# A graph attention phase with one masked leaky score array, a mask made on ScalarE, and a new order on all engines

## The reference, cut to what matters

```python
h = relu(layernorm(x)); h = h + emb_table[node_type]
for t in range(3):
    xw = h @ W[t]; a_s = xw @ att_src[t]; a_d = xw @ att_dst[t]
    e = leaky_relu(a_s[src] + a_d[dst], 0.2)            # edges of type t only
    m = max(segment_max(e, dst), leaky_relu(a_s + a_d))
    w = exp(e - m[dst]); w_self = exp(leaky_relu(a_s + a_d) - m)
    out += (segment_sum(w * xw[src]) + w_self * xw) / (segment_sum(w) + w_self) + bias[t]
x = x + out
x = x + update(segment_sum((relu(layernorm(x))[src] @ dW + db) * filters(edge_attr)))
```

## Time and profile before

| what | value |
|---|---|
| median of 3 runs | 4670.54 us (4664.35 to 4681.23) |
| profiled execution: its time, its span | 4672.4 us, 4670.4 us |
| mean granted TensorE clock | 0.633 |
| busy: PE, PEld, DVE, ACT, POOL | 89%, 69%, 56%, 27%, 69% |
| attention phase, first to last look at a unit's maximum | 131.2 us to 2429.3 us |

### The profile page before, as it was taken

The page is one execution under the profiler, slowest core; times in us unless marked ns, Lnnn a source line. Parts: engine busy times, 40 slices in busy tenths (PEclk is TensorE's granted clock), DMA queues, the critical chain, the costliest instruction groups (busy, mean ns, idle before and its releaser), DMA issues. The chain is left out here.

```text
span 4670.4 us, 64104 instructions
## 1 busy us (share of the span) xinstructions
PE 4157.6 (89%) x18574; PEld 3219.4 (69%) x18575; DVE 2604.0 (56%) x6278; ACT 1242.0 (27%) x3966; POOL 3241.2 (69%) x3261
## 2 busy tenths in 40 slices
PE   7899999999999999999987689888888899888998
PEld 5676767767777777777766567776676677767776
DVE  6777777777777777777774333333333333333333
ACT  4433333333333333333331111111111111111111
POOL 3777777777777777777740577777777777777774
PEclk9656565566665556655666666666666666666667
DMA  2222222222222222222224222222222222222223
GB/s 80 50 50 48 48 48 48 48 48 48 48 48 48 48 47 48 48 48 48 48 29 130 66 73 74 73 73 74 73 74 72 74 74 73 74 73 74 73 74 75
DMA packets 215747, 288.25 MB, mean 62 GB/s; under 512 B 136194, under 2 KB 143930, under 8 KB 215723
## 3 DMA queue, kind: packets, MB, share of 16 engines
q0 software_dynamic: 105472, 222.39, 21.0%
q1 hardware_dynamic: 110250, 65.57, 5.1%
HBM read 277.81 MB, written 9.81 MB: 62 GB/s over the span
## 5 line engine op out<-in xcount | busy, mean ns | idle before, releaser
L54 POOL DMA_INDIRECT ae_xg<-table,ae_idx x1620 | 1677.2, 1035 | 640.9 <-issue 456.2
L54 POOL DMA_INDIRECT ce_xg<-table,ce_idx x1620 | 1534.1, 947 | 499.8 <-issue 493.4
L1042 DVE TENSOR_TENSOR ce_ps_f<-ce_ps_f,ce_fb 128x768 f32<-128x768 f32 x270 | 260.9, 966 | 1288.9 <-PE ce_ps_f L995 1288.9
L1014 PE MATMUL ce_ps_h<-ce_ea,ce_fw 50*128 50x384 f32 x1080 | 638.1, 731 | 247.1 <-DMA ce_ea<-in_edge_attr 246.6
L551 PE MATMUL ae_ps_a<-ae_e,ae_xg 128*128 128x96 f32 x3240 | 772.0, 402 | 63.5 <-DVE ae_e L662 63.5
L995 PEld LDWEIGHTS ce_ps_f<-ce_fw,ce_hid 128*128 128x128 f32 x3240 | 642.9, 301 | 239.5 <-issue 239.0
L551 PEld LDWEIGHTS ae_ps_a<-ae_e,ae_xg 128*128 128x128 f32 x3240 | 651.0, 293 | 164.0 <-DVE ae_e L662 88.1
L975 ACT ACTIVATE ce_hid<-ce_ps_h,ce_fb 128x768 f32<-128x768 f32 x270 | 243.1, 900 | 1782.8 <-PE ce_ps_h L1014 1782.8
L995 PE MATMUL ce_ps_f<-ce_fw,ce_hid 128*128 128x128 f32 x3240 | 715.9, 403 | 0.0
L512 ACT ACTIVATE ae_e<-ae_e,ae_sc 128x96 f32<-128x96 f32 x1620 | 459.7, 362 | 957.2 <-DVE ae_e L654 957.2
L555 PE MATMUL ae_ps_d<-ae_e,cst 128*1 128x96 f32 x3240 | 551.4, 356 | 0.0
(11 more groups left out here) (141 smaller groups left out, 3654.8 us busy)
## 6 DMA issues: line engine op xcount, KB each, us to landing
ce_ea<-in_edge_attr SPq DMA_DIRECT2D x270, 150.0 KB
ae_xg<-table,ae_idx POOLq DMA_INDIRECT x1620, 2.6
ce_xg<-table,ce_idx POOLq DMA_INDIRECT x1620, 2.6
fa_inv_den<-rden SPq DMA_DIRECT2D x7, 1344.0 KB, 7.6
ae_idx<-in_src SPq DMA_DIRECT2D x276, 3.0 KB, 1.6
ce_idx<-in_src SPq DMA_DIRECT2D x276, 3.0 KB, 1.6
table<-pr_rows POOLq DMA_DIRECT2D x7, 462.0 KB, 4.1
pr_x<-in_x SPq DMA_DIRECT2D x7, 448.0 KB, 3.3
```

The costliest lines, as they stand in the source:

```text
L54: eng.indirect_dma_start(out=out, out_offset=None, in_=table[:, :], in_offset=bass.IndirectOffsetOnAxis(ap=idx, axis=0)).then_inc(done, 16)
L1014: last = nc.tensor.matmul(ps_h[:, k * 512:k * 512 + H], fw1[:, :], ea[:, s % XS, k * H:(k + 1) * H], start=True, stop=True)
L1042: nc.vector.tensor_tensor(filt, filt, fb2[:, :].unsqueeze(1).to_broadcast([P, CH, D]), ALU.add).then_inc(s_bias, 1)
```

## The change

Three things change in the attention phase, and nothing in the other phases.

First, there is one score array. `e` = leaky(sc + dst - off) is made once per unit; the maximum is the maximum of this array, and the exponential is that of this array less the new maximum. ACT writes sc + dst into PSUM (`ps_y`, L538, six instructions, PSUM to PSUM), DVE subtracts `off` in place (L677), ACT makes 0.8 relu of it into `upper` (L529, one instruction over 576 numbers), DVE adds 0.2 of the array (L682), reduces it to `high` (L687), and later adds minus the maximum (L709); ACT takes one exponential over all 576 numbers (L519). Foreign keys stand at about -1e30 throughout, so nothing is masked after the exponential. PE spreads only the destination's score (L610) and one row with the new maximum and the rise side by side (L621, one matmul of 192 columns), and spreads the highest score without adding the destination's (L615).

Second, ACT makes `off`: the square of 2^50 (iota - key), six instructions per unit (L546), each with its bias column chosen by a register; `start_pass` writes the keys in that form (`less_key`, f32). The denominators' matmuls (L597) write into the bank of the sums.

Third, all four streams are ordered anew. On PE, a step holds the highest row, the maxima and the sums of unit n - 2, the denominators of n - 3 in two halves, the target row of n and the transpose of n - 1.

```diff
         @block.scalar
-                    for c in range(CH):
-                        nc.scalar.activation(by_chunk[b][:, c, :], by_chunk[b][:, c, :], ACT.Exp, bias=sc2[:, b, c:c + 1])
-                    act.wait_ge(s_fall, n)
-                    nc.scalar.activation(rescale[:, b, :], ps_d[b][:, KEYS:2 * KEYS], ACT.Exp).then_inc(s_e, 1)
+                    nc.scalar.activation(e[:, s % 3, :], e[:, s % 3, :], ACT.Exp).then_inc(s_e, 1)
+
+                def rescales(n):
+
+                    act.wait_ge(s_less, n)
+                    nc.scalar.activation(rescale, rescale, ACT.Exp).then_inc(s_rescale, 1)
+
+                def uppers(n):
+
+                    act.wait_ge(s_masked, n)
+                    nc.scalar.activation(upper[:, :].rearrange("p (h k) -> p h k", h=2), scores, ACT.Relu, scale=1.0 - SLOPE).then_inc(s_upper, 1)
...
+                    for c in range(CH):
+                        last = nc.scalar.activation(off[:, s % 2, c, :], h.iota, ACT.Square, bias=keys[:, c:c + 1], scale=STEP)
...
         @block.tensor
+                def maxima(n):
+
+                    pe.wait_ge(s_rise, n)
+                    nc.tensor.matmul(ps_m[:, 0:2 * KEYS], h.less_row32[0:64, :], rise[:, :, :].rearrange("p a k -> p (a k)"),
+                                     start=True, stop=True).then_inc(s_less, 1)
...
         @block.vector
+                def subtract(n, s):
+
+                    dve.wait_ge(s_rescale, n)
+                    nc.vector.tensor_tensor(by_chunk[s % 3], by_chunk[s % 3], less_max.unsqueeze(1).to_broadcast([P, CH, KEYS]),
+                                            ALU.add).then_inc(s_sub, 1)
```

More of the change, by code:

```diff
@@ L521, in turn @@
-                        if not (first and s < 2):
-                            act.wait_ge(s_sum, n - 2)
-                        act.wait_ge(s_dst, n)
-                        act.wait_ge(s_score, n)
-                        for c in range(CH):
-                            last = nc.scalar.activation(by_chunk[b][:, c, :], ps_c[b][:, 0:KEYS], ACT.Relu, bias=sc[:, b, c:c + 1])
-                        last.then_inc(s_pre, 1)
-                turns(act, turn)
-                exps((r + 1) * NU, SL - 1)
+                        n = (r * TURNS + i) * SL + s + 1
@@ L532, in _ @@
+                n = (r + 1) * NU
+                rescales(n - 1)
+                uppers(n)
+                exps(n - 1, SL - 2)
+                rescales(n)
+                exps(n, SL - 1)
         @block.tensor
@@ L560, in turn @@
                     for s in range(SL):
-                        n, b = (r * TURNS + i) * SL + s + 1, s % 2
-                        lag1 = not (first and s < 1)
-                        pe.wait_ge(s_high, n)
-                        nc.tensor.transpose(ps_t[0:KEYS, 0:P], high[:, :], h.ident).then_inc(s_turned, 1)
-                        nc.tensor.matmul(kv(ps_c[b][:, 0:KEYS]), h.ones[0:1, :], state[0:1, :, bass.ds(base[s], W)], start=True, stop=True)
-                        nc.tensor.matmul(kv(ps_c[b][:, KEYS:2 * KEYS]), h.slope[0:1, :], state[0:1, :, bass.ds(base[s], W)], start=True, stop=False).then_inc(s_dst, 1)
@@ new lines, in turn @@
+                        lag1, lag2, lag3 = (not (first and s < k) for k in (1, 2, 3))
+                        if lag2:
+                            highest_row(n - 2)
+                        if lag3:
+                            totals(n - 3, s - 3, range(0, CH // 2))
+                        if lag2:
+                            maxima(n - 2)
+                        if lag3:
+                            totals(n - 3, s - 3, range(CH // 2, CH))
+                        targets(n, base[s], first and s == 0)
@@ L583, in _ @@
+                        if lag2:
+                            sums(n - 2, s - 2, first and s < 4)
+                        if lag1:
+                            turned(n - 1)
                 pe.wait_ge(key_ready, r + 1)
@@ L665, in scale_sums @@
-                def scale_sums(n, s, base, fresh):
+                    new, fall = rise[32:33, 0, :], rise[32:33, 1, :]
+                    if not fresh:
+                        dve.wait_ge(s_max, n - 1)
+                    dve.wait_ge(s_z, n)
+                    nc.vector.tensor_tensor(kv(new), kv(ps_z[32:33, 0:KEYS]), m, ALU.max).then_inc(s_new, 1)
+                    dve.wait_ge(s_new, n)
+                    nc.vector.tensor_tensor(kv(fall), kv(new), m, ALU.subtract).then_inc(s_rise, 1)
```

244 lines of the change are left out of this document (117 added, 127 removed).

## The result

| | median us | lowest to highest | ratio to before (95%) |
|---|---|---|---|
| before, same chip | 4670.4 | 4664.35 to 4681.23 | |
| changed | 4537.5 | 4533.58 to 4541.97 | 0.971 (0.969 to 0.973) |

The change is 133 us faster, where 36 were forecast (4634), inside the range but 97 us off. The profiled execution took 4533.6 us with a span of 4531.9.

A forecast was written before the change was run, and what follows sets the result against it. The prediction took TensorE's stream at 1.2 GHz as the present bound (8.54 us a step) and a ring of waits as the new one: 8.27 + 0.09 + 0.03 = 8.39 us, giving 4634 us, range 4510 to 4712.

The forecast's parts named there:

- the ring: Attention-phase chain of waits from transpose through DVE, TensorE and ACT back to transpose, priced at 8.27 us at 1.2 GHz.
- sums twice 1.53 = 3.06: TensorE's sums matmuls ahead of the transpose, priced as two halves of 1.53 us each, 3.06 us.
- the reserve: Allowance of 0.03 us added to each attention step for errors in the six handovers between engines, giving 8.39 us.
- the head of a turn: DVE's register load at each turn's start, said to stick out about 0.55 us in six steps, 0.09 a step.
- the second rival: Slower: longer waits ahead of highest row and sums, clock low; 8.83 us a step, 4750 us, or 4710 at two thirds; chance 0.12.
- TensorE's own stream: TensorE's matmuls and transpose in one attention step, said to total 7.3 us at 1.2 GHz, against 8.6 before.
- The clock: TensorE was to stay at 1.2 GHz in nearly all of the attention phase, granted clock near 0.50.
- The first rival: TensorE's clock keeps rising as often as before (granted 0.60): step 8.0 us, 146 us less, 4528 us; chance 0.22.
- Its signs: Attention-phase profile readings expected if right: clock 0.50 to 0.52, TensorE's two waits, L687 starts 8.4 us apart, POOL waiting longer.
- POOL's floor: POOL's gathers with their issue take 7.81 us a unit, so no step averages less; 4480 us the least.
- What stays under cover: DVE's and ACT's other work in a step, 5.5 and about 5.0 us busy, said not to set the step.
- the convolution: The phase outside attention, priced at no change since none of its instructions moved.

The follow-up runs named there:

- e1: The changed kernel with TensorE's sums again in two halves of three matmuls, the target row between them: 4742.95 us, ratio 1.0145 to the kernel before.
- e14: The kernel before with both halves of its sums (L551) in one run behind the maxima L579 and L580: 5070.88 us, ratio 1.0856.
- e3: The changed kernel with TensorE's register load at a turn's head moved to just ahead of the first target row: 4519.2 us, ratio 0.9661.
- e4: The changed kernel with the exponential as six instructions of 96 numbers instead of one of 576: 4634.48 us, ratio 0.9908.
- e13: The changed kernel with the mask made on VectorE in two instructions of 288 numbers, not ACT's six L546: 4534.85 us, ratio 0.9701.
- e11: The changed kernel with TensorE's order as in e12, VectorE's order left as it was: 4634.49 us, ratio 0.9894.
- e12: The changed kernel, TensorE reordered with denominators in one run straight before sums, VectorE's leaky array and maximum ahead of merge and scale: 4388.55 us, ratio 0.9371.
- e10: The kernel of e12 with TensorE's register load moved to just ahead of a turn's first target row: 4386.22 us, ratio 0.9366.
- e5 to e8: Kernels of e13, e10, e12 with e13's mask, and e11, on a chip taking 5556 us for the kernel before: 5499.5, 5442.1, 5445.9, 5447.9 us.

## Why the prediction was wrong

**The step that failed** is the term of the ring "sums twice 1.53 = 3.06". They measure 2.67 us. The 1.53 was read from a half that stood between other matmuls, and doubling it charged the break between two halves that the new order does not have. e1 splits the difference: put back as halves, the sums take 2.90; one run saves 0.23 of it. The rest, 0.16, is the change to the next instruction: the last half takes 1.38 ahead of the transpose and 1.52 ahead of the target row, so the 1.53, read ahead of L555, was too dear there as well. In the kernel before the same step shows (e14): 2.81 us for one run ahead of L555. 0.39 us a step is 105 us, a little more than the miss: with 0.02 for the other terms and 0.03 for the reserve, less 0.08 for the head of a turn, the step came out 0.36 us shorter than forecast, and 0.36 x 270 = 97 us.

The other terms, with what they measured:

| term | priced | measured |
|---|---|---|
| transpose to L691, L691, handover | 0.48, 0.29, 0.06 | 0.46, 0.29, 0.05 |
| highest row, half of the denominators | 0.51, 1.00 | 0.51, 1.05 |
| maxima to their end, rescale | 1.02, 0.23 | 1.00, 0.23 |
| subtraction, exponential | 0.75, 0.65 | 0.76, 0.68 |
| three handovers, last handover | 0.12, 0.10 | 0.11, 0.05 |
| sums | 3.06 | 2.67 |
| ring | 8.27 | 7.86 |
| head of a turn, a step | 0.09 | 0.17 |
| reserve for handovers | 0.03 | 0 |
| step | 8.39 | 8.03 |

7.86 + 0.17 is 8.03, and so is (2296.0 - 135.6)/269. The steps with a turn's head take 8.85 us in the mean, 0.99 over the ring. **The head of a turn** was priced with VectorE's load alone, 0.55 us where 0.66 stuck out; TensorE's own load adds 0.47 us in half of the turns (the second rival's place, without its size), and e3 takes that back. The head was too cheap by 0.08 us a step, which hid part of the error in the sums.

**TensorE's own stream** was forecast at 7.3 us, and 7.86 less the two waits of 0.38 and 0.18 is 7.30. That agreement is luck: the denominators took 2.10 instead of 2.0, the maxima 0.94 to the next start instead of 0.81, the target row 0.67 instead of 0.5, and the sums 0.39 less than priced. The maxima's price per column was read from L1014, in another phase, and it was too low.

**The clock** was called rightly: 0.50 throughout. The first rival, a clock that keeps rising, gave 4528 us and came closest to the time, and it is wrong: the phase has not one stretch at 2.4 GHz. A time near a rival's is no evidence for it; the granted clock is. The prediction's reason for the low clock, that no dense stretch of sums and denominators is left, fits the other runs: with the denominators cut in two by the maxima (e1, e3, e4, e13) the granted clock of the attention phase is 0.50, and where denominators and sums stand back to back it is 0.62 (e11) and 0.67 (e12). No run changed that stretch and nothing else.

**Its signs.** TensorE waits 0.38 us ahead of L615 (0.5 said) and 0.18 ahead of L591 (0.4 to 0.5 said); L687's starts are 8.03 us apart (8.4 said); ACT is early at L524, 3.19 us. POOL's wait for L591 was to grow and fell, from 154.8 us to 61.2.

**The second rival** needed 0.90 for the exponential and 0.15 for the last handover; they are 0.68 and 0.05. **POOL's floor** of 7.81 us a unit was wrong as well, without effect at a step of 8.03: it took the gathers' 1026 ns as theirs, and 82 ns of it was VectorE's two-operand work. At 7.49 it became the bound as soon as the ring was shorter (e12). **What stays under cover** held: the mask costs nothing on either engine, neither as six short activations of ACT nor as VectorE's 0.92 us (e13). The maximum L687 had less room than said: it ended at 1412.98, 0.26 us ahead of the transpose, where the prediction left 0.8. And the convolution did not move (clock 0.6 to 0.7 after the phase, as before).

Where the 133 us came from, as far as shown: a ring of 7.86 us sets the step instead of TensorE's full stream of 8.6 us. Taking single parts out of the changed kernel costs 0.77 us a step for the unbroken sums outside the target row (e1, 206 us), 0.36 for the single exponential (e4), and nothing for the mask's move (e13). These prices hold inside the new order and do not add up to the gain over the old one, which no experiment took apart. What the second level of the clock was worth to the kernel before was not measured by itself.

The best version is that of e12, or of e10, which can't be told from it: 4386 to 4388 us, 6% under the kernel before.

## What to carry to other kernels

Price a group of matmuls by how it will stand: whole if it runs whole, and with what follows it; a half doubled charges a break that isn't there. Before an instruction is moved on one engine, look for who waits for its end (e11, e14): one and the same order on TensorE gave 4634 or 4388 us by what VectorE did first (e11, e12). A longer or shorter ring changes only the steps in which it is the last to arrive: here a sixth of the steps, those with a register load, hid what was added. And before an engine's mean duration is used as a floor, look at the ones above the mean: the gathers took 1026 ns in the mean and 944 undisturbed, and a quarter of them was being held by another engine.

## What the runs showed of the hardware

A gather that starts while VectorE reads two SBUF operands stands nearly until VectorE is done, and ends 0.81 to 0.83 us after it (1.41 and 1.35 us long against 0.94, 490 gathers in three runs); with one of the operands in PSUM it does not (0.96 us at most). Six activations of 96 numbers overlap to 1.15 us (e4). Twelve instructions of f32 matmul take, at 1.2 GHz and to the next start, 2.67 us ahead of the transpose and 2.81 ahead of the denominators in one run, and 2.90 (e1) and 3.06 in two halves. And of the chips used, one took 5556 us for the kernel before; the gathers themselves took 943 to 951 ns there (e5 to e8), with a wait of 2.1 us ahead of one in six.
